# k's high part against q's high part, q's low part and the identity in one product of 384 columns

## The reference

```python
q, k, v = [gelu(xn @ W1 + b1) @ W2 + b2 for each of q, k, v]     # xn = layernorm(x)
scores = einsum('bid,bjd->bij', q, k) / scale
scores = scores * tril(ones(T, T))                               # the causal mask
out = einsum('bij,bjd->bid', scores, v)
x = x + layernorm(out) * ln_w + ln_b
idx = argmax(pe @ sign(tile_sigs).T)                             # one of 8 tiles, by position alone
x = x + layernorm(x) @ W[idx].T + b[idx]
```

## Time and profile before

| | |
|---|---|
| time, median of 3 runs | 304.71 us (304.62 to 305.18) |
| the profiled execution | 304.78 us |
| its span | 303.0 us |
| mean granted TensorE clock | 0.992 |
| PE busy | 281.8 us (93%) |
| VectorE busy | 237.2 us (78%) |
| ScalarE busy | 191.6 us (63%) |
| GpSimd busy | 168.1 us (55%) |

### The profile page before, as it was taken

One profiled execution on the slowest core, in us unless ns is written; L12 is line 12 of the kernel. 1 busy time (PEld: TensorE's weight loads), 2 busy tenths in 40 slices (PEclk: granted clock), 3 DMA queues, 4 the chain that ended last, 5 costly groups with the idle time before them and its releaser, 6 DMA issues.

```text
span 303.0 us, 5527 instructions
## 1 busy us (share of the span) xinstructions
PE 281.8 (93%) x1818; PEld 252.7 (83%) x1818; DVE 237.2 (78%) x549; ACT 191.6 (63%) x389; POOL 168.1 (55%) x230
## 2 busy tenths in 40 slices
PE   6869999999899999999999999999999898999970
PEld 6757988898789889888978898989898898999850
DVE  4587879889988978986898689678856879867660
ACT  2278568767666776678667866876877445787000
POOL 3902452172459184937554663648374476777771
PEclk9999999999999999999999999999999999999996
DMA  7816991002111211021121100017021460693220
GB/s 199 285 53 175 358 294 35 0 2 69 35 39 37 80 63 38 6 100 39 38 88 52 68 7 0 21 56 203 2 92 37 128 194 24 191 299 107 70 69 19
DMA packets 24193, 27.83 MB, mean 92 GB/s; under 512 B 4643, under 2 KB 22052, under 8 KB 24102
## 3 DMA queue, kind: packets, MB, share of 16 engines
q1 hardware_dynamic: 15750, 13.29, 15.0%
q0 software_dynamic: 3296, 8.64, 8.2%
q10 hardware_dynamic: 5120, 5.55, 5.8%
HBM read 13.95 MB, written 14.44 MB: 94 GB/s over the span
## 4 chain that ended last, share of the span: by engine, by line
PE 68%; DVE 13%; DMA 5%; POOL 4%; issue 4%; ACT 2%; SPq 1%; POOLq 0%; DVEq 0%; ACTq 0%
PE ring L475 40%; PE o_ps L475 10%; PE s_ps L475 6%; POOL out_dram L1697 3%; DMA w_stage<-w1v 3%; PE w_ps L475 2%; DMA slot_rows<-sorted_rows 2%; PE ring L488 2%; PE sc_ps L571 2%; DVE xres L1185 1%; DVE xnT L1113 1%; PE sc_ps L569 1%; DVE st L1192 1%; PE w_ps L614 1%; DVE w_sp L1329 1%
## 5 line engine op out<-in xcount | busy, mean ns | idle before, releaser
L475 PE MATMUL ring<-xnT,w_sp 128*128 128x512 f32 x288 | 73.4, 399 | 5.5 <-DVE hT L1118 3.5
L475 PEld LDWEIGHTS ring<-xnT,w_sp 128*128 128x128 f32 x288 | 51.9, 189 | 17.8 <-DVE hT L1118 4.8
L850 ACT ACTIVATE ring<-ring,b_cols 128x512 f32<-128x512 f32 x48 | 31.7, 660 | 24.8 <-PE ring L475 23.9
L475 PE MATMUL ring<-hT,w_sp 128*128 128x512 f32 x192 | 46.4, 396 | 0.0
L475 PEld LDWEIGHTS ring<-hT,w_sp 128*128 128x128 f32 x192 | 35.4, 188 | 8.1 <-DVE hT L1118 0.2
L1118 DVE TENSOR_TENSOR hT<-ring,hT 128x512 fp32r<-128x512 f32 x48 | 32.4, 680 | 12.3 <-ACT hT L853 12.0
L1650 POOL DMA_INDIRECT sorted_rows<-xres,slot_i x30 | 31.2, 1041 | 8.4 <-issue 6.6
L1616 POOL TENSOR_TENSOR vtok<-v,vtok 128x512 fp32r<-128x512 f32 x14 | 17.9, 1287 | 28.6 <-ACT vtok L870 28.6
L1597 POOL TENSOR_SCALAR nm<-mv 128x4 f32<-128x4 f32 x8 | 1.8, 231 | 52.2 <-DVE mv L1100 52.2
L853 ACT CAST hT<-ring 128x512 fp32r<-128x512 f32 x48 | 28.2, 587 | 1.5
L1697 POOL DMA_INDIRECT out_dram<-slot_rows x22 | 21.6, 981 | 6.7 <-issue 6.1
(11 more groups left out here) (238 smaller groups left out, 679.7 us busy)
## 6 DMA issues: line engine op xcount, KB each, us to landing
sorted_rows<-blank ACTq DMA_DIRECT2D x1, 5032.0 KB, 19.1
xt<-x SPq DMA_DIRECT2D x8, 512.0 KB, 3.6
slot_rows<-sorted_rows SPq DMA_DIRECT2D x22, 136.0 KB, 3.1
w_stage<-tile_w SPq DMA_DIRECT2D x8, 256.0 KB, 2.9
h<-sorted_rows SPq DMA_DIRECT2D x15, 136.0 KB, 3.1
hT<-position_table POOLq DMA_DIRECT2D x1, 512.0 KB, 8.1
sorted_rows<-xres,slot_i POOLq DMA_INDIRECT x30, 2.5
row_stage<-rows ACTq DMA_DIRECT2D x1, 384.0 KB, 8.1
```

The lines of the kernel that those rows point to most:

```text
L475: last = te.matmul(o, lhs[k][a], rhs[k][c], start=start and k == 0 and i == 0, stop=stop and k == n - 1 and i == 2, skip_group_check=check)
L850: nc.scalar.activation(full, ring[(2 + m) % 3][:, :], ACT.Gelu, bias=b1c[:, m // 2, m % 2:m % 2 + 1]).then_inc(gelu, 1)
```

## The change

`q_eye` and `q_low` become one tile `q_all` of three blocks of 128 columns a chunk and half: identity, high, low for the first half of the features, and high, low, identity for the second. k's high part meets all three blocks in one product of 384 columns. The bank has four blocks: ktok's first half, high scores, partial scores (k high x q low), ktok's second half. The order of the blocks makes the 384 columns of each half land on neighbouring blocks of the bank. k's low part still has 256 columns, now picked with a stride. So the scores lie in two blocks: ScalarE copies the partial one to SBUF (`sc_part`) after ktok, VectorE adds it to the other one, and masks all four chunks in one instruction (`scores_masked`) ahead of `xnT_rest`. VectorE's work on a chunk now waits for that copy (`sc_parted`); PE's two waits for read banks go to the sum (`sc_sum`). In PE's list `back_scores` of chunk 0 moves behind part 1 of `front_h`, except in the last round, and in VectorE's list `out_centred` of chunk 0 moves behind the first `h_rest`, in the last round ahead of it. GpSimd writes the identities in two instructions.

```diff
--- before.py
+++ after.py
@@ -121,8 +121,8 @@
         v32 = sb("v32", [P, CH, C])
         sc32 = sb("sc32", [P, GT])
         xnT = sb("xnT", [P, 2, KC, GT], F32R)
-        q_eye = sb("q_eye", [P, KC, CH, 2, P], F32R)
-        q_low = sb("q_low", [P, KC, CH, P], F32R)
+        q_all = sb("q_all", [P, KC, CH, 3, P], F32R)
+        sc_part = sb("sc_part", [P, GT])
         kT = sb("kT", [P, 2, KC, GT], F32R)
         ktok = sb("ktok", [P, 2, CH, C], F32R)
         vtok = sb("vtok", [P, 2, CH, C], F32R)
@@ -191,6 +191,8 @@
         ktok_lo = sem("ktok_lo")
         scores = sem("scores")
         sc_mask = sem("sc_mask")
+        sc_parted = sem("sc_parted")
+        sc_sum = sem("sc_sum")
         sc_hi = sem("sc_hi")
         sc_lo = sem("sc_lo")
@@ -327,11 +329,16 @@
         kept = [sc_ps, w_ps, ring[2], sc_ps]
+        HI, LO, EYE = (1, 0), (2, 1), (0, 2)
+
         def q_chunk(k, c):
-            return [q_eye[:, k, c, 0, :], q_low[:, k, c, :]]
+            return [q_all[:, k, c, HI[k], :], q_all[:, k, c, LO[k], :]]
         def q_from(k, j):
-            return [q_eye[:, k, j:CH, 0, :], q_low[:, k, j:CH, :]]
+            return [q_all[:, k, j:CH, HI[k], :], q_all[:, k, j:CH, LO[k], :]]
+
+        def kept_k(c):
+            return kept[c][:, :].rearrange("p (a n) -> p a n", a=4)[:, 0:4:3, :]
         off_at = [0, 3 * P, 5 * P]
         sc_off = ktok[:, :, :, :].rearrange("p a c d -> p a (c d)")
@@ -510,7 +517,7 @@
                     if m >= 3:
                         bank_free(s, m - 3)
                     elif m == 0 and s:
-                        te.wait_ge(sc_mask, CH * s - 1)
+                        te.wait_ge(sc_sum, CH * s - 1)
                     if first and m % 2 == 0:
                         te.wait_ge(w_lo, m // 2 + 1)
                     for k in range(KC):
@@ -555,21 +562,20 @@
                 te.wait_ge(q_lo, 2 * s + 2)
                 te.wait_ge(k_lo, 2 * s + 2)
                 if s == 0:
-                    te.wait_ge(eye_set, 1)
+                    te.wait_ge(eye_set, 2)
                 else:
                     te.wait_ge(wf_lo, tiles_turned(s))
                 for c in range(CH):
                     if c == CH - 1:
-                        te.wait_ge(sc_mask, CH * s + 1)
-                    o = kept[c][:, 0:P]
-                    both = kept[c][:, :].rearrange("p (a n) -> p a n", a=2)
+                        te.wait_ge(sc_sum, CH * s + 1)
+                    bank = kept[c][:, :].rearrange("p (a n) -> p a n", a=4)
                     for k in range(KC):
-                        wide = both[:, :, 0:P] if k else kept[c][:, 0:2 * P].rearrange("p (a n) -> p a n", a=2)
                         k_hi_c, k_lo_c = [kT[:, a, k, cols(c)] for a in range(2)]
-                        te.matmul(wide, k_hi_c, q_eye[:, k, c], start=k == 0, stop=False, skip_group_check=True)
-                        te.matmul(o, k_hi_c, q_low[:, k, c, :], start=False, stop=False, skip_group_check=True)
-                        last = te.matmul(wide, k_lo_c, q_eye[:, k, c], start=False, stop=k == KC - 1,
-                                         skip_group_check=True)
+                        te.matmul(bank[:, k:k + 3, :], k_hi_c, q_all[:, k, c], start=k == 0, stop=False,
+                                  skip_group_check=True)
+                        these = bank[:, 1:4:2, :] if k else bank[:, 0:2, :]
+                        q_and_eye = q_all[:, k, c, 0:3:2, :] if k else q_all[:, k, c, 0:2, :]
+                        last = te.matmul(these, k_lo_c, q_and_eye, start=False, stop=k == KC - 1, skip_group_check=True)
                     last.then_inc(scores, 1)
             def back_chunk(s, c):
@@ -751,9 +757,8 @@
             for s in range(LAST - 1):
                 front_transposes(s + 1, False)
                 back_state(s, 0)
-                front_h(s + 1, (0,), False)
+                front_h(s + 1, (0, 1), False)
                 back_scores(s, 0)
-                front_h(s + 1, (1,), False)
                 back_chunk(s, 1)
                 front_h(s + 1, (2, 3), False)
                 if s == 3:
@@ -856,7 +861,7 @@
                 if j == 0:
                     act.wait_ge(o_ready, CH * s)
                 act.wait_ge(fill, FILLS * s + 9 + j)
-                nc.scalar.activation(q_eye[:, j, :, 0, :], ring[(8 + j) % 3][:, :].rearrange("p (c n) -> p c n", c=CH),
+                nc.scalar.activation(q_all[:, j, :, HI[j], :], ring[(8 + j) % 3][:, :].rearrange("p (c n) -> p c n", c=CH),
                                      ACT.Identity,
                                      bias=b2c[:, Q, j:j + 1]).then_inc(q_hi, 1)
@@ -871,14 +876,17 @@
             def scores_rounded(s):
                 if s < LAST:
-                    act.wait_ge(sc_mask, CH * s + CH)
+                    act.wait_ge(sc_mask, s + 1)
                 else:
                     act.wait_ge(diagonal, CH - 1)
                 nc.scalar.copy(scT[:, 0, :], sc32[:, :]).then_inc(sc_hi, 1)
             def ktok_rounded(s, c):
                 act.wait_ge(scores, CH * s + c + 1)
-                nc.scalar.copy(ktok[:, 0, c, :], kept[c][:, P:P + C]).then_inc(ktok_hi, 1)
+                nc.scalar.copy(ktok[:, 0, c, :].rearrange("p (a n) -> p a n", a=2), kept_k(c)).then_inc(ktok_hi, 1)
+                if s and c == 0:
+                    act.wait_ge(sc_sum, CH * s)
+                nc.scalar.copy(sc_part[:, cols(c)], kept[c][:, 2 * P:3 * P]).then_inc(sc_parted, 1)
             def state_rounded(s, c):
                 if state_kept(s, c):
@@ -1121,8 +1129,8 @@
             def q_rest(s, js=(0, 1)):
                 for j in js:
                     dve.wait_ge(q_hi, 2 * s + 1 + j)
-                    nc.vector.scalar_tensor_tensor(out=q_low[:, j], in0=ring[(8 + j) % 3][:, :].rearrange("p (c n) -> p c n", c=CH),
-                                                   scalar=b2c[:, Q, j:j + 1], in1=q_eye[:, j, :, 0, :].bitcast(F32),
+                    nc.vector.scalar_tensor_tensor(out=q_all[:, j, :, LO[j], :], in0=ring[(8 + j) % 3][:, :].rearrange("p (c n) -> p c n", c=CH),
+                                                   scalar=b2c[:, Q, j:j + 1], in1=q_all[:, j, :, HI[j], :].bitcast(F32),
                                                    op0=ALU.add, op1=ALU.subtract).then_inc(q_lo, 1)
             def k_rest(s, j):
@@ -1132,10 +1140,18 @@
                                                op0=ALU.add, op1=ALU.subtract).then_inc(k_lo, 1)
             def chunk_rest(s, c):
-                dve.wait_ge(ktok_hi, CH * s + c + 1)
-                nc.vector.tensor_tensor(ktok[:, 1, c, :], kept[c][:, P:P + C], ktok[:, 0, c, :].bitcast(F32),
+                dve.wait_ge(sc_parted, CH * s + c + 1)
+                nc.vector.tensor_tensor(ktok[:, 1, c, :].rearrange("p (a n) -> p a n", a=2), kept_k(c),
+                                        ktok[:, 0, c, :].bitcast(F32).rearrange("p (a n) -> p a n", a=2),
                                         ALU.subtract).then_inc(ktok_lo, 1)
-                nc.vector.tensor_tensor(sc32[:, cols(c)], kept[c][:, 0:P], tril[:, :], ALU.mult).then_inc(sc_mask, 1)
+                nc.vector.tensor_tensor(sc32[:, cols(c)], kept[c][:, P:2 * P], sc_part[:, cols(c)],
+                                        ALU.add).then_inc(sc_sum, 1)
+
+            def scores_masked(s):
+                dve.wait_ge(sc_sum, CH * s + CH)
+                nc.vector.tensor_tensor(sc32[:, :].rearrange("p (c i) -> p c i", c=CH),
+                                        sc32[:, :].rearrange("p (c i) -> p c i", c=CH),
+                                        tril[:, :].unsqueeze(1).broadcast_to([P, CH, P]), ALU.mult).then_inc(sc_mask, 1)
             def v_biased(s, j):
                 dve.wait_ge(fill, FILLS * s + 13 + j)
@@ -1381,10 +1397,10 @@
             dve.wait_ge(consts, 4)
             for c in range(CH):
                 chunk_rest(0, c)
+            scores_masked(0)
             xnT_rest(1)
             scores_rest(0)
             state_rest(0, 0)
-            out_centred(0, 0)
             def slot_rest(n):
                 dve.wait_ge(xb_hi, n + 1)
@@ -1443,6 +1459,7 @@
             for s in range(LAST - 1):
                 h_rest(s + 1, 0)
+                out_centred(s, 0)
                 if s:
                     x1_stats(s - 1, range(CH))
                 h_rest(s + 1, 1)
@@ -1489,16 +1506,17 @@
                 v_biased(s + 1, 1)
                 for c in range(CH):
                     chunk_rest(s + 1, c)
+                scores_masked(s + 1)
                 xnT_rest(s + 2)
                 scores_rest(s + 1)
                 state_rest(s + 1, 0)
                 x1_final(s, (3,))
-                out_centred(s + 1, 0)
             s = LAST - 1
             dve.wait_ge(fill, FILLS * LAST + 2)
             nc.vector.memset(xn[:, :, C - 1:C], 1.0).then_inc(ones_set, 1)
+            out_centred(s, 0)
             h_rest(LAST, 0)
             x1_stats(s - 1, range(CH))
             tile_rest(NT - 1)
```

(5 more changed lines are left out.)

## The result

The changed kernel takes 312.51 us (median of 4, 311.92 to 314.13) against 304.83 of the kernel before in the same sessions: a ratio of 1.0249 (1.0222 to 1.0275). It is slower by 2.5%. The forecast was 311.5 with a range of 307.0 to 313.9, so time and direction hold. The span of the profiled execution went from 303.0 to 310.2 us.

What follows compares the result with a forecast made beforehand. PE, busy 281.8 of 303.0 us, was the bound. Hand-overs, the stretches after the products of groups 0 to 6, cost 0.75 + 0.95 + 0.7 + 3.6 (3 to 5) + 0.8 = 6.8 us: 311.5 us, range 307.0 to 313.9.

Steps and rivals of the forecast that it cites:

- PE's pace and the fourth chunk: Score chunks take 0.58 us instead of 0.70, but the fourth waits for its bank; 0.04 us left per hand-over.
- The mask ahead of xnT: VectorE's added mask precedes xnT's low halves; unhindered, it starts xnT's low half 0.75 us later and front_h 0.53 later.
- the 5.2 that would have refuted the forecast: PE's front_h starting within 5.2 us of the scores would prove the forecast wrong.
- the 1.4 us that the forecast named as its own sign: xnT's first low half on VectorE comes 1.4 us later against the start of the scores than before.
- rival (a): GpSimd does not hold VectorE's mask; PE is late by 0.6 us a hand-over instead of 1.3: 309.0 us, chance 0.27.
- How long GpSimd holds the mask: VectorE's mask waits until 0.19 us before the end of GpSimd's second TENSOR_SCALAR: 0.69 us, the upper end.
- The moved back_scores hides this: Residual sum holds the scores' low half, done at 69.83; PE's moved back_scores comes only at 70.7.
- Hand-over 6: After group 6's products, unmoved back_scores waits 1.6 us for late scores; PE's idle takes up half: 0.8 us.
- tile numbers: PE's sequencer loads in groups 4 to 6, put behind the wait for xnT by the reorder: 0.1 us won.
- (b): VectorE writes xnT's low half no later than wanted, so PE's pace decides: 300.5 us, chance 0.07.
- (c): VectorE becomes the bound; every hand-over costs the full 1.3 us, the last 1.6: 314.1 us, chance 0.12.
- (d): Gain and wait cancel: strided products gain and the fourth chunk does not wait: 304.7 us, chance 0.04.

Runs made afterwards that it cites:

- Runs 2 and 9: Shorter products alone on the kernel before, one score term left out: 303.65 us, ratio 0.9953; 9 adds an own bank for the fourth chunk: ratio 0.9947.
- run 6: Changed kernel, mask still ahead of xnT, with GpSimd writing zeros instead of the residual sum: ratio 1.0026 to the kernel before.
- its control: Kernel before with only the back_scores and out_centred moves, and GpSimd writing zeros instead of the residual sum: ratio 0.9874.
- Run 7: Changed kernel with the mask behind xnT_rest and GpSimd writing zeros instead of the residual sum: ratio 0.9875 to the kernel before.
- run 11: Complete changed kernel with the mask on GpSimd and an own bank for the fourth chunk: 315.53 us against 317.17, ratio 0.995.
- run 5: Changed kernel with the mask behind xnT_rest and GpSimd's residual sum moved to mid-step in steps 3 to 5 alone: ratio 1.0133.
- runs 11 and 12: Both are complete changed kernels with the mask on GpSimd: with an own bank for the fourth chunk, ratio 0.995; without it, 0.9978.

## Why the prediction was right, and where it was not

**PE's pace and the fourth chunk.** Right: 0.29 us for half a chunk, and the wait for the bank lets the fourth chunk start at 2.03 (forecast 2.13); the transposes gain 0.05 us (0.04). Runs 2 and 9 show both parts of it: the products gain when alone, and more when the fourth chunk has a bank of its own.

**The mask ahead of xnT.** Right as the main term. front_h starts 5.60 to 5.91 us behind the scores, outside the 5.2 that would have refuted the forecast; run 6 against its control puts 4.75 us of six steps on the mask. Run 7 shows that nothing is left once the mask is late and GpSimd reads nothing. But xnT's low half starts only 0.7 to 1.0 us later against the scores: the 1.4 us that the forecast named as its own sign came nowhere, and at five of seven hand-overs it is the 0.75 of rival (a).

**How long GpSimd holds the mask: mis-sized.** The step took it as held until 0.19 us before the end of the second TENSOR_SCALAR, 0.69 us at five hand-overs. Measured: held at two, for 0.27 to 0.31 us. The mask ends at 67.23; if it then ran at its plain 0.69, it ran from 66.54, while the TENSOR_SCALAR goes on to 67.16. The carrying over from L1185 and from the CAST beside L1329, which were held nearly to GpSimd's end, was the error; the working had seen that the two starts lie 0.05 us apart, but took one outcome as certain.

**The low half of the scores, held by the residual sum.** The mechanism holds at hand-overs 1 to 6 (2.03 to 2.93 us, x1_final free). "The moved back_scores hides this" failed at hand-over 2: the mask came first, pushed GpSimd, and the residual sum started 0.01 us ahead of the low half (98.47, 98.48):

```profile
98.48 2.93 DVE L1164 TENSOR_TENSOR scT<-sc,scT 128x512 fp32r<-128x512 f32 x1
...
98.47 2.40 POOL L1627 TENSOR_TENSOR xres<-xt,row_stage 128x1024 f32<-128x1024 f32 x1
...
101.47 0.62 PE L482 MATMUL o_ps<-vtok,scT 128*128 128x256 f32 x3 [0.31 <-DVE scT L1164]
```

The forecast had no term for it there, and 0.7 us in all; it cost 1.47. In run 6, where the low half is free, the same step took 28.63 us instead of 29.52, so 0.9 of it is the hold. At hand-overs 4 and 5 the hold also reached PE, through the low half of the state behind it, which the working had as early enough. VectorE and PE at hand-over 4:

```profile
160.00 0.68 DVE L1173 TENSOR_TENSOR state<-s_ps,state 128x512 fp32r<-128x512 f32 x1
...
160.82 0.71 PE L482 MATMUL o_ps<-state,q_all 128*128 128x256 f32 x4
```

PE's product that reads the state starts 0.14 us after VectorE's end, and 0.35 behind the product before it instead of 0.12.

**Hand-over 6: mis-sized.** Forecast 1.6 less 0.8 taken up by an idle stretch; measured 1.77, with nothing of it taken up. back_scores waits 1.19 us:

```profile
217.23 0.60 PE L620 MATMUL w_ps<-ident,w_stage 128*128 128x128 f32 x4
219.02 0.63 PE L482 MATMUL o_ps<-vtok,scT 128*128 128x256 f32 x3 [1.19 <-DVE scT L1164]
```

The working had left out that in this round out_centred stands ahead of the first h_rest and waits for those scores. h_rest so starts at 10.07 us behind the scores instead of 8.74: VectorE is late by 1.3 itself, so PE's later wait for VectorE (0.8 us, still in the list of waits) is not shortened. This is read from the timelines; no run changes that order.

**The sum.** Too high by 1.2 us at hand-overs 1 and 3 to 5, where mask and tile numbers were charged in full; too low by 0.8 at hand-over 2 and by 1.0 at 6. 6.8 against 7.1: that the total is so close is luck, as the errors of the parts cancel.

**The rivals.** (a) had the mask free of GpSimd, which was so at five of seven hand-overs, but missed that the pushed GpSimd then holds the scores longer; its 309.0 is too low by that and by hand-over 6. (b) would need VectorE unhindered: run 11 comes nearest, with a bank of its own besides, and gains 1.6 us by the medians, not 4.2. (c) is excluded by the table (0.75 to 0.89 us at five of the hand-overs, not 1.3) and by run 5. (d) had the fourth chunk not wait: it waits.

## What to carry to other kernels

A shortened product pays only as far as the next reader lets it: look for the wait that the long version covered (here a bank read 0.17 us ahead of its reuse). Look also for what an added instruction stands ahead of in its engine's list. Before adding a VectorE instruction with two SBUF inputs, look at what GpSimd has in flight at that time; moving either one moves the wait, so choose the place by both lists, or, as in runs 11 and 12, give the work to GpSimd itself. Starts 0.05 us apart are to be forecast as two outcomes.

## What was not expected of the hardware

GpSimd's TENSOR_SCALAR of 128x255 (0.93 us) holds a VectorE instruction for about 0.3 us only, though the residual sum (2.4 us) and the CAST hold it nearly to their end. Where the mask goes free, the TENSOR_SCALAR is lengthened by 0.4 to 0.5 us (0.93 to between 1.30 and 1.44). Which of the two it is does not show in the recorded starts when they lie within 0.06 us. A VectorE instruction of 128x16 was lengthened from 0.16 to 2.37 us. The Trainium skill (SBUF — State Buffer, "SBUF: two separate sides") has whichever of the two engines starts first keep the shared ports for its whole instruction. The rows agree for the residual sum, beside which the low half of the scores took 2.03 to 2.93 us instead of 0.68; they do not for the TENSOR_SCALAR (0.3 of its 0.93 us), where the measurement decides. A select of 128x512 on GpSimd took 0.64 us, no more than VectorE's mask of the same shape.
